# x also laid out by columns: W_q centred on chip, and each row's reciprocal deviation multiplied into q as VectorE reads it out of PSUM

## What is computed

```python
def _layernorm(x, axis=-1, eps=1e-05):
    m = jnp.mean(x, axis=axis, keepdims=True)
    v = jnp.var(x, axis=axis, keepdims=True)
    return (x - m) / jnp.sqrt(v + eps)
...
q = x_q @ W_q.T + b_q            # x_q = _layernorm(x)
k = x_kv @ W_k.T + b_k           # x_kv = ctx_1024
v = x_kv @ W_v.T + b_v
scores = jnp.einsum('bhqd,bhkd->bhqk', qh, kh) * scale
attn = jax.nn.softmax(scores, axis=-1)
ctx = jnp.einsum('bhqk,bhkd->bhqd', attn, vh)
...
x = x + ctx @ W_out.T + b_out
x = x + experts(_layernorm(x))   # top 2 of 8, silu(a) * g, weighted sum
```

## Time and profile before

| what | value |
|---|---|
| median of three runs | 1176.52 us |
| the profiled execution | 1174.99 us, its span from the first to the last instruction 1173.2 us |
| PE, PEld, DVE, ACT, POOL busy | 1136.0, 1018.2, 941.5, 774.8, 597.5 us |
| stage one | the first 530 us: slot 0 begins at 24.86 us |
| median from issue to landing, x tile of 128 KB and context group of 512 KB | 2.4 and 4.5 us |
| slots 4 to 54, scores to scores | 7.76 us each, 7.88 where q = 1 |

### The profile page before, as it was taken

The page is one execution under the profiler, slowest core; times in us unless marked ns, Lnnn a source line. Parts: engine busy times, 40 slices in busy tenths (PEclk is TensorE's granted clock), DMA queues, the critical chain, the costliest instruction groups (busy, mean ns, idle before and its releaser), DMA issues. The chain is left out here.

```text
span 1173.2 us, 38427 instructions
## 1 busy us (share of the span) xinstructions
PE 1136.0 (97%) x12514; PEld 1018.2 (87%) x12515; DVE 941.5 (80%) x2949; ACT 774.8 (66%) x1635; POOL 597.5 (51%) x729
## 2 busy tenths in 40 slices
PE   6999999999999999988999999999999999999995
PEld 4677777777777777777999999999999999999995
DVE  6789999999999999898888877776776777677772
ACT  5677777777777776666766766666666666666652
POOL 6345677767766776595564333333333333333333
PEclk9999999999999999999999999999999999999998
DMA  5123333333333333536787776777777777767743
GB/s 191 36 74 94 110 106 100 113 113 104 104 109 113 111 102 105 188 127 215 191 221 201 200 212 171 217 195 190 189 210 200 172 198 210 192 172 214 194 109 68
DMA packets 106631, 180.18 MB, mean 154 GB/s; under 512 B 14400, under 2 KB 80128, under 8 KB 106368
## 3 DMA queue, kind: packets, MB, share of 16 engines
q1 hardware_dynamic: 74448, 136.54, 36.4%
q0 software_dynamic: 25584, 35.54, 16.0%
q10 hardware_dynamic: 6464, 6.36, 1.7%
HBM read 132.57 MB, written 45.29 MB: 152 GB/s over the span
## 5 line engine op out<-in xcount | busy, mean ns | idle before, releaser
L1782 POOL DMA_INDIRECT out_rows<-y_gated,block_tokens x114 | 187.2, 1642 | 257.3 <-DMA out_rows<-y_gated,block_tokens 107.4
L675 PE MATMUL bank<-block_T_hi,w_hi 128*128 128x256 f32 x912 | 261.1, 286 | 0.7 <-DVE block_T_lo L1397 0.7
L677 PE MATMUL bank<-block_T_hi,w_lo 128*128 128x256 f32 x912 | 256.1, 281 | 0.0
L676 PE MATMUL bank<-block_T_lo,w_hi 128*128 128x256 f32 x912 | 256.1, 281 | 0.0
L839 ACT ACTIVATE probs_T<-bank 128x512 f32<-128x512 f32 x256 | 132.1, 603 | 64.7 <-PE bank L512 64.7
L675 PEld LDWEIGHTS bank<-block_T_hi,w_hi 128*128 128x128 f32 x912 | 173.9, 191 | 0.9 <-DVE block_T_lo L1397 0.9
L676 PEld LDWEIGHTS bank<-block_T_lo,w_hi 128*128 128x128 f32 x912 | 173.2, 190 | 0.0
L677 PEld LDWEIGHTS bank<-block_T_hi,w_lo 128*128 128x128 f32 x912 | 172.9, 190 | 0.0
L1095 DVE TENSOR_REDUCE row_max<-bank 128x4 f32<-128x512 f32 x256 | 157.9, 675 | 13.0 <-PE bank L493 13.0
L1715 POOL DMA_INDIRECT routed_rows<-rows,dest_i x128 | 129.7, 1013 | 37.3 <-issue 33.4
L1380 DVE TENSOR_TENSOR w_lo<-w_raw,w_hi 128x1024 fp32r<-128x1024 f32 x114 | 134.1, 1218 | 6.2 <-ACT w_hi L940 6.2
(11 more groups left out here) (211 smaller groups left out, 2941.0 us busy)
## 6 DMA issues: line engine op xcount, KB each, us to landing
w_raw<-in_L_ffn_W SPq DMA_DIRECT2D x114, 512.0 KB, 4.7
half_w<-in_L_ffn_W SPq DMA_DIRECT2D x42, 512.0 KB, 5.6
block_rows<-routed_rows SPq DMA_DIRECT2D x57, 272.0 KB, 4.8
x_in<-in_x SPq DMA_DIRECT2D x64, 128.0 KB, 2.4
ctx_T<-in_ctx SPq DMA_DIRECT2D x16, 512.0 KB, 4.5
x_res<-in_x SPq DMA_DIRECT2D x64, 128.0 KB, 2.6
out_rows<-x SPq DMA_DIRECT2D x64, 128.0 KB, 2.3
w_lo<-in_L_ffn_W ACTq DMA_DIRECT2D x8, 512.0 KB, 4.4
```

Of the source, the lines that this page charges most:

```text
L675: mm(dst, w1h[k][:, c, at:at + P], xh[:, k, c, :], start=(c == 0), stop=False)
L676: mm(dst, w1h[k][:, c, at:at + P], xl[:, k, c, :], start=False, stop=False)
L677: last = mm(dst, w1l[k][:, c, at:at + P], xh[:, k, c, :], start=False, stop=(c == KC - 1))
L1782: nc.gpsimd.indirect_dma_start(out=out[:, :], out_offset=bass.IndirectOffsetOnAxis(ap=tk[:, u % U, t:t + 1], axis=0), in_=yg[:, u % 2, t, ...
```

## The change

x comes in a second time, with columns on the partitions (`x_T`, laid out on the host as the context already is), so that nothing transposes it. The layer norm is taken out of x and put into q: (x - m) W = x (W - mean of W's rows), so W_q is centred once on the chip (a product with a matrix of 1/256 gives the column means, VectorE subtracts them out of PSUM), and the reciprocal deviation of a row is a factor of its column of the transposed q. For that the 512 factors of a group are stored to DRAM by SyncE (ScalarE's queue for groups 0 and 1) and read back to all 128 partitions (`store_rstd`, `load_rstd`); VectorE multiplies them with q out of bank 5 (`q_scaled`), and ScalarE adds the bias in place (`q_bias`). The high part of x_T is made by ScalarE from SBUF, 128x512 at a time, the low part by GpSimd (by VectorE for groups 0 and 1). The statistics of two tiles stand in slots q = 2 and q = 3, where they stood in q = 1 and q = 3. `ln1_norm`, `to_T` and two of GpSimd's three operations are gone.

The diff, cut to its core (the orders of `before()` on VectorE and ScalarE are shown below as they come out):

```diff
--- before.py
+++ after.py
+    rr = nc.dram_tensor("rstd_rows", (NB // GB, GB * P), F32, kind="Internal").ap()
...
+        (rb, avg), (w1l0,) = overlaid(
+            "rstd_rows_then_w1_lo",
+            [("ln1_rstd_rows", [P, 2, GB * P], F32), ("average", [P, P], F32)],
+            [("w1_lo0", [P, KC, 2 * F], F32R)])
...
+        def store_rstd(eng, g):
+            eng.wait_ge(s_rs1, 2 * (g + 1))
+            if g > 0:
+                eng.wait_ge(s_rst, g * 16)
+            eng.dma_start(rr[g].rearrange("(p q) -> p q", p=P), rs1[:, g % 2, :]).then_inc(s_rst, 16)
+
+        def load_rstd(eng, g):
+            eng.wait_ge(s_rst, (g + 1) * 16)
+            if g > 0:
+                eng.wait_ge(s_rld, g * 16)
+            if g >= 2:
+                eng.wait_ge(s_qm, 2 * (g - 1))
+            eng.dma_start(rb[:, g % 2, :], rr[g].rearrange("(o n) -> o n", o=1).to_broadcast([P, GB * P])).then_inc(s_rld, 16)
...
+            def load_xt(g):
+                if g >= 4:
+                    sp.wait_ge(s_xlp, KC * (g - 3))
+                elif g >= 2:
+                    sp.wait_ge(s_xl, KC * (g - 1))
+                sp.dma_start(xt_in[:, g % 2], xT[g]).then_inc(s_ldt[g % 2], 16)
+
             def before():
+                load_xt(0)
                 for t in range(4):
                     load_x(t)
+                load_c(0)
                 sp.dma_start(consts[:], cst).then_inc(s_const, 16)
-                load_c(0)
                 for t in range(4, LB):
                     load_x(t)
+                load_xt(1)
                 load_c(1)
                 for dst, b in ((bob, bo), (brb, br)):
                     sp.dma_start(dst[:], b.rearrange("(o n) -> o n", o=1).to_broadcast([P, b.shape[0]])).then_inc(s_w, 16)
                 for t in range(LB, LB + 6):
                     load_x(t)
                 load_c(2)
+                load_xt(2)
+                load_xt(3)
...
+                if t % GB == 0 and real(t + 2 * GB):
+                    store_rstd(sp, t // GB + 2)
+                if t % GB == 1 and real(t + 2 * GB):
+                    load_rstd(sp, t // GB + 2)
+                if t % GB == 3 and real(t + 4 * GB):
+                    load_xt(t // GB + 4)
...
-            def to_T(t, bk):
-
-                pe.wait_ge(s_xn, count(t))
-                for c in range(KC):
-                    last = nc.tensor.transpose(bk[:, c * P:(c + 1) * P], xn[:, t % LB, c * P:(c + 1) * P], ident)
-                last.then_inc(s_xT, 1)
-
             def qk_proj(g, o, bk):
 
                 par = g % 2
-                if o == 0:
-                    pe.wait_ge(s_xl, GB * (g + 1))
+                if o == 0 and g < 2:
+                    pe.wait_ge(s_xl, KC * (g + 1))
+                if o == 0 and g >= 2:
+                    pe.wait_ge(s_xlp, KC * (g - 1))
...
+                pe.wait_ge(s_zro, 1)
+                pe.wait_ge(s_wn[0], 16)
+                for c in range(KC):
+                    last = mm(bank[3][:, 0:D], avg[:], w_in[:, 0, c, :], start=(c == 0), stop=(c == KC - 1))
+                last.then_inc(s_wm, 1)
+                for o in range(4):
+                    if o % 2 == 0:
+                        pe.wait_ge(s_wl, o // 2 + 1)
+                    qk_proj(0, o, bank[4 + o])
+                pe.wait_ge(s_wl, 3)
+                for q in (2, 3, 0, 1):
+                    if q < 2:
+                        pe.wait_ge(s_qm, q + 1)
+                    else:
+                        pe.wait_ge(s_ev, q - 1)
+                    v_proj(q, bank[4 + q])
                 pe.wait_ge(s_const, 16)
-                for q in range(GB):
-                    to_T(q, bank[q])
-                pe.wait_ge(s_wl, 2)
-                for o in range(4):
-                    qk_proj(0, o, bank[4 + o])
-                for q in range(GB):
-                    pe.wait_ge(s_xl, q + 1)
-                    to_T(GB + q, bank[q])
-                pe.wait_ge(s_wl, 4)
-                for q in range(GB):
-                    pe.wait_ge(s_ev, q + 1)
-                    v_proj(q, bank[4 + q])
-                pe.wait_ge(s_v, GB)
-                pe.wait_ge(s_xl, LB)
...
-                    to_T(LB, bank[6])
+                    pe.wait_ge(s_v, GB)
                     pe.wait_ge(s_bvr, 1)
+                    pe.wait_ge(s_wl, 4)
...
-                    pe.wait_ge(s_ev, min(GB + t + 1, NB))
+                    if real(GB * g) and q < 2:
+                        pe.wait_ge(s_qm, 2 * g + q + 1)
+                    else:
+                        pe.wait_ge(s_ev, min(GB + t + 1, NB))
...
-                if real(t + 9):
-                    pe.wait_ge(s_xl, t + 9)
-                    to_T(t + 9, bank[6])
...
-            def xT_hi(t, bk):
-                q, par = t % GB, (t // GB) % 2
-                act.wait_ge(s_xT, count(t))
-                if q == 0 and real(t - LB):
-                    act.wait_ge(s_qk, GB * (t // GB - 1))
-                nc.scalar.activation(t_hi[:, par, 0:KC, q * P:(q + 1) * P],
-                                     bk[:, 0:D].rearrange("p (c n) -> p c n", c=KC), ACT.Copy).then_inc(s_xh, 1)
+            def xT_hi(g, c):
+                act.wait_ge(s_ldt[g % 2], (g // 2 + 1) * 16)
+                if g >= 2:
+                    act.wait_ge(s_qk, GB * (g - 2) + 2)
+                nc.scalar.activation(t_hi[:, g % 2, c, :], xt_in[:, g % 2, c, :], ACT.Copy).then_inc(s_xh, 1)
 
...
+            def q_bias(g, o):
+                act.wait_ge(s_qm, 2 * g + o + 1)
+                dst = qT0[:, g % 3, :] if o == 0 else qT1[:, g % 2, :]
+                nc.scalar.activation(dst, dst, ACT.Identity, bias=bqc[:, o:o + 1]).then_inc(s_ev, 1)
...
-            def ln1_norm(t):
-
-                k, h = (t // 2) % 2, t % 2
-                act.wait_ge(s_rs1, pairs(t))
-                if real(t - LB):
-                    act.wait_ge(s_xT, count(t - LB))
-                nc.scalar.activation(xn[:, t % LB, :], x_in[:, t % LB, :], ACT.Identity,
-                                     bias=nb1[:, k, h:h + 1], scale=rs1[:, k, h:h + 1]).then_inc(s_xn, 1)
...
-                if real(t + 9):
-                    xT_hi(t + 9, bank[6])
                 if q % 2 == 0 and real(GB * (g + 1)):
                     ctx_hi(g + 1, q // 2)
-                if real(t + 10):
-                    ln1_norm(t + 10)
+                if q == 3 and real(GB * (g + 2)):
+                    xT_hi(g + 2, 0)
+                if q == 1 and real(GB * (g + 1)):
+                    xT_hi(g + 1, 1)
+                if real(GB * g) and q < 2:
+                    q_bias(g, q)
...
-            def xT_lo(t, bk):
-                q, par = t % GB, (t // GB) % 2
-                dve.wait_ge(s_xh, count(t))
-                V.tensor_tensor(t_lo[:, par, 0:KC, q * P:(q + 1) * P], bk[:, 0:D].rearrange("p (c n) -> p c n", c=KC),
-                                t_hi[:, par, 0:KC, q * P:(q + 1) * P].bitcast(F32), ALU.subtract).then_inc(s_xl, 1)
+            def xT_lo(g, c):
+                dve.wait_ge(s_xh, KC * g + c + 1)
+                V.tensor_tensor(t_lo[:, g % 2, c, :], xt_in[:, g % 2, c, :], t_hi[:, g % 2, c, :].bitcast(F32),
+                                ALU.subtract).then_inc(s_xl, 1)
+
+            def q_scaled(g, o, bk):
+
+                dve.wait_ge(s_qk, GB * g + o + 1)
+                dve.wait_ge(s_rld, (g + 1) * 16)
+                if o == 0 and g >= 3:
+                    dve.wait_ge(s_st, GB * (g - 2) * NCH)
+                if o == 1 and g >= 2:
+                    dve.wait_ge(s_st, GB * (g - 1) * NCH)
+                dst = qT0[:, g % 3, :] if o == 0 else qT1[:, g % 2, :]
+                V.tensor_tensor(dst.rearrange("m (q p) -> m q p", q=GB), bk[:, :].rearrange("m (q p) -> m q p", q=GB),
+                                rb[:, g % 2, :].rearrange("m (p q) -> m q p", q=GB), ALU.mult).then_inc(s_qm, 1)
...
+                dve.wait_ge(s_wm, 1)
+                V.tensor_tensor(w_in[:, 0], w_in[:, 0],
+                                bank[3][:, 0:D].rearrange("p (o n) -> p o n", o=1).to_broadcast([P, KC, D]),
+                                ALU.subtract).then_inc(s_wc, 1)
+                for c in range(KC):
+                    xT_lo(0, c)
+                dve.wait_ge(s_wc, 1)
+                w_part_lo(0)
+                w_part_lo(1)
...
-                if real(t + 8):
-                    xT_lo(t + 8, bank[6])
+                if q < 2 and real(GB * (t // GB + 1)):
+                    q_scaled(t // GB + 1, q, bank[5])
...
-                if t % 2 == 1 and real(t + 11):
+                if q == 2 and real(t + 10):
+                    ln1_stats(t + 10)
+                if q == 3 and real(t + 11):
...
-                n, k = pairs(t), (t // 2) % 2
-                if n > 2:
-                    pool.wait_ge(s_xn, 2 * (n - 2))
-                rstd(s_ve1, s_pr1, s_rs1, n, ve1[:], mv1[:, :, 0], 2, nm1[:], rs1[:, k], nb1[:, k])
+                n, g, q = pairs(t), t // GB, t % GB
+                if g >= 2:
```

(10 more changed lines are left out.)

124 lines of the change are left out of this document (59 added, 65 removed).

## The result

The changed kernel took 1202.63 us, the median of 4 runs (1199.35 to 1205.39); beside it the kernel before took 1177.44. The ratio is 1.0217, with a 95% interval from 1.0189 to 1.0244: 2.2% slower, against a forecast of 1179.3 us and a range that ended at 1185.5. The profiled execution took 1203.37 us with a span of 1201.1, which is 27.9 more than before.

A forecast was written before the change was run, and what follows sets the result against it. The prediction took the wait for ScalarE's exponentials, not TensorE's busy time, to bound the steady slots. Steady part 0 and start +2.8 us, set against the median of 1176.52, gave 1179.3 us; range 1175.5 to 1185.5.

The forecast's parts named there:

- The steady part of TensorE: Slots 0 to 54: removing transposes of 0.37 us each, covered by the wait for ScalarE's exponentials, is worth 0.
- taken as 0.65, so every slot still fits: VectorE, two 128x512 q_scaled per group: 0.65 us each, bounds 0.6 and 1.3; steady slots get no longer, worth 0.
- the slack of 0.31 us: VectorE's free time at the end of slot q = 0, said to hold the 0.3 us more that this slot gets.
- VectorE overflows in slots q = 0: Rival: q_scaled takes 1.3 us, 0.35 us reaches line 507, 15 times, 5.2 us in all, giving 1184.5 us; 14%.
- the margin, taken as 0.44 less 0.13: Between the end of VectorE's maxima and TensorE's line 507: 0.44 us, less 0.13 for the semaphore, absorbs lateness.
- the two casts of the start: VectorE casts in the start: 0.4 us for both with GpSimd idle, against 1.33 beside it; bounds 0.3 and 2.7.
- The start: Before the steady slots: maxima of slot 0 begin at 28.85 instead of 26.02 us, a delay of 2.8 passed on whole.
- First projection: In the start, after loads and low parts: 13.5 us, bounds 12.8 to 14.6, against 13.29 before.
- The third projection: In the start, TensorE's first half of k: done at 19.2 us, from where ScalarE's chain of copies runs.
- The 5.73 us for eighteen matmuls: In the start: time from the first to the nineteenth matmul in the profile before, used to place the third projection.
- GpSimd and SyncE: Steady slots: 1.3 us of added low part on GpSimd and one more DMA in three slots of four cost 0.
- Stage two is bound by itself: Stage two, after stage one's slots: its length is taken as unchanged, with no term in the sum.

The follow-up runs named there:

- contig_b: Changed kernel with reciprocals stored so that they come back in the column order of q and q_scaled reads them with step 1; 1301.46 us, ratio 1.1082.
- no_transposes_b: Kernel before without the two transposes of x per slot from tile 9 on; 1176.87 us against 1176.49, ratio 1.0001.
- before_scatter_first: Kernel before with GpSimd's low part of ctx_T behind its two scatters in slots q = 1 and 3 instead of ahead; 1207.28 us, ratio 1.0262.
- before_odd64_b: Kernel before with 64 unused bytes ahead of w1_raw1, moving w1_hi1, w1_lo1 and activations to 64 modulo 128; 1194.34 us against 1203.1, ratio 0.9924.

## Why the prediction was wrong

**The steady part of TensorE: right.** The 55 pairs of transposes lay in front of a wait; taking them out gave 0, measured alone (ratio 1.0001) and within the change (waits for probs_T from 0.2 to 20.4 us, slots q = 2 and 3 unchanged).

**The failed step: `q_scaled` "taken as 0.65, so every slot still fits".** Two things were wrong with it. First the size: the forecast had given both bounds, 0.6 and 1.3, and named the step of four floats as what would decide, then took the row of the same width that reads with step 1. It measured 1.08 with the step, 0.69 without. Second, and worth more, the slack of 0.31 us was read as time that could be filled, with nothing said on what stands beside it. The carries are the last VectorE work of the slot; 0.68 us later they stand beside ctxT_lo and x_res_bo and lose another 0.93. So the rival "VectorE overflows in slots q = 0" had the right place and was given 14% and 5.2 us; it cost some 12 (12.1 us in slots q = 1 and 1.4 in q = 0, of which 1.7 belong to the fallen clock), because a slot went up by 0.95 us and not by 0.35. Of the margin, taken as 0.44 less 0.13, 0.34 was found. The forecast knew the effect (it priced the two casts of the start by it, and rightly) and didn't carry it over to the place where the change moved two-operand work. contig_b shows that even with 0.65 the forecast would have been wrong: the maxima began 2.08 us behind the scores there, 0.92 later than before, and less the 0.34 that cost nothing that is an estimate of 0.6 us a slot.

**The start: right in kind, 1.5 us short.** The forecast was 2.8, it was 4.3. First projection 13.45 for 13.5, casts 0.22 each for 0.4 together. The third projection came 1.4 us late: the granted clock stood at 0.5 until 19.3 us, where before it rose at 16.5, and the eighteen matmuls took 6.93 us. TensorE had stood idle for 6.25 us ahead of the first of them, before for 2.07. The 5.73 us for eighteen matmuls were an interval with the higher clock in it. That moved the copies of k and all behind them; together with the late maxima (1.1 us behind the forecast) `q_scaled`, on the path to slot 1 with 1.07 us instead of 0.65, makes the 1.5.

**GpSimd and SyncE: 0 was right for their own queues in the profiled execution.** No DMA of the maxima came late. What GpSimd's added 1.28 us do through VectorE had not been asked.

**Stage two: not seen.** "Stage two is bound by itself" took its pace as given. The diff drops three small tiles and moves w1_lo0; that was in the text of the change, and the stage took 6.9 us more. The trace of before held a hint: its even blocks, with w1 at 64, ran at 0.118 us a matmul, its odd ones, with w1 at 0, at 0.120 and 0.123.

**The clock.** Four stretches of 3.4 us at half the clock, 1.2 us each in the slots, are part of the lengths above and were in no term. What brought them isn't shown. In contig_b, where TensorE stood for 7 us in each group, the clock fell in each group; in no_transposes_b, with 35.8 us of short waits, and in before_scatter_first, with slots of 9.1 us, it stayed at 1.00 up to slot 55 and beyond.

## What to carry to other kernels

Before pricing an instruction that is taken out, look whether it stands in front of a wait: the transposes were 20 us of TensorE and worth nothing. When work is added to VectorE, price each operand by its step, and look at what GpSimd does at the new time of everything behind it: here instructions with two SBUF operands, a tensor_scalar and casts out of SBUF lost time beside a GpSimd one, however small they were, and maxima out of PSUM did not. After any change of the tiles compare the pace of stages whose code didn't change; an address may have moved.

## What the runs showed of the hardware

- VectorE beside GpSimd, medians of the changed kernel's trace up to 560 us: a 128x2 tensor_scalar out of SBUF 0.17 us alone, 0.69 beside a GpSimd tensor_tensor; a carry 0.16 and 0.60; a 128x16 scalar_tensor_tensor 0.18 alone and 1.63 in the row above; the maxima out of PSUM 0.68 and 0.68; and, in the kernel before, statistics 0.41 and 0.41. The Trainium skill (SBUF — State Buffer, "SBUF: two separate sides") says that the two engines share a pair of ports that one of them holds for the whole of its instruction. The trace agrees: the carries ended within 0.02 us of the end of GpSimd's second instruction.
- TensorE's pace depended on where in SBUF tiles stand: in the first products of stage two 0.120 to 0.123 us a matmul with both operands at 0 modulo 128 bytes, 0.113 to 0.121 with one at 64. 22.61 against 23.35 us for the same instructions is 3%.
- A DMA of 512 single elements took 10.9 us to land, and a 4 KB DMA issued behind it on the same queue landed no earlier.
- The same kernel took 1176 us in some series of runs and 1203 to 1207 in others, with a mean granted clock of 0.99 to 1.00 in both. The exponentials began 1.5 to 1.7 us behind the first transposed scores in before_odd64_b, 0.64 to 0.66 behind the end of GpSimd's second scatter, and 1.09 behind the scores in the kernel before as profiled. What does that is open. It isn't the chip that decides: chip 10 gave 1176 us in one series and 1203 in another.
